# Cross-attention with a small expert layer: where the key weights are split, six stage slots for the last key tiles, waits per bank and per block

## The reference, cut to what matters

```python
q = (layernorm(x) @ Wq + bq).reshape(B, L, NKV, G, HDIM)     # 8 groups of 4 heads, width 128
k_, v_ = jnp.split(ctx @ Wkv + bkv, 2, axis=-1)              # 8 key/value heads
scores = jnp.einsum('blkgd,bmkd->bkglm', q, k) * scale       # each block of 64 sees its own 64
o = jnp.einsum('bkglm,bmkd->blkgd', softmax(scores), v)
x = x + o @ Wo + bo
x = x + top-2-of-8 experts of rank 16 (layernorm(x)) * 0.5
```

## Time and profile before

| what | value |
|---|---|
| timed runs | 1084.54, 1086.21, 1086.89 us (median 1086.21) |
| profiled execution | span 1083.3 us, first to last instruction; the profile has no other time of it |
| TensorE busy | 1043.1 us, 96% of the span |
| VectorE, GpSimd, ScalarE busy | 807.1 us (75%), 674.0 us (62%), 556.9 us (51%) |
| chain that ended last | TensorE 83%, VectorE 7%, DMA 5%, GpSimd 2% |
| slices of the span with TensorE below 8 tenths | the first and the last |
| DMA | 183 GB/s on average, up to 327 GB/s in a slice of the start |

### The profile page before, as it was taken

The page is one execution under the profiler, slowest core; times in us unless marked ns, Lnnn a source line. Parts: engine busy times, 40 slices in busy tenths (PEclk is TensorE's granted clock), DMA queues, the critical chain, the costliest instruction groups (busy, mean ns, idle before and its releaser), DMA issues.

```text
span 1083.3 us, 17308 instructions
## 1 busy us (share of the span) xinstructions
PE 1043.1 (96%) x5409; PEld 856.0 (79%) x5409; DVE 807.1 (75%) x1420; ACT 556.9 (51%) x1314; POOL 674.0 (62%) x563
## 2 busy tenths in 40 slices
PE   7999899888999999999999999999999999999996
PEld 6788687776778888888888888888888888887884
DVE  3554355446997798788879887887888797788886
ACT  3032203225775675667566656756666665566420
POOL 0285235766886787578667866876786678575300
PEclk9999999988999999999999999999999999999998
DMA  8636863875654637273635637282736456350003
GB/s 300 194 121 205 327 185 110 312 248 214 223 199 161 243 108 292 97 288 111 246 141 209 231 127 254 97 321 93 261 138 221 161 194 250 103 156 11 2 37 120
DMA packets 85658, 197.99 MB, mean 183 GB/s; under 512 B 10561, under 2 KB 43369, under 8 KB 70385
## 3 DMA queue, kind: packets, MB, share of 16 engines
q1 hardware_dynamic: 83072, 181.73, 48.1%
q10 hardware_dynamic: 2544, 15.73, 3.7%
HBM read 161.78 MB, written 35.65 MB: 182 GB/s over the span
## 4 chain that ended last, share of the span: by engine, by line
PE 83%; DVE 7%; DMA 5%; POOL 2%; SPq 1%; ACT 1%; issue 1%; DVEq 0%; ACTq 0%
PE banks L1633 25%; PE banks L1634 23%; PE banks L1635 23%; PE banks L1773 5%; PE banks L1756 3%; PE banks L1757 3%; DMA raw<-in_L_xattn_Wkv_dram 2%; DMA keys_dram<-parts 1%; PE banks L1658 1%; DMA xo<-x_dram 1%; DVE stats L1193 1%; DVE xo L1118 1%; SPq L402 1%; DMA v_raw<-values_dram 1%; DVE y L1313 1%
## 5 line engine op out<-in xcount | busy, mean ns | idle before, releaser
L1633 PE MATMUL banks<-wo_h,xo 128*128 128x512 f32 x512 | 204.5, 399 | 0.0
L1634 PE MATMUL banks<-wo_l,xo 128*128 128x512 f32 x512 | 200.4, 391 | 0.0
L1635 PE MATMUL banks<-wo_h,xo 128*128 128x512 f32 x512 | 199.8, 390 | 0.0
L562 POOL TENSOR_TENSOR qT_l<-parts,qT_h 128x512 fp32r<-128x512 f32 x128 | 165.3, 1298 | 46.8 <-ACT qT_h L784 46.8
L1633 PE MATMUL banks<-xo,w_h 128*128 128x512 f32 x448 | 180.5, 403 | 12.2 <-DVE parts L1157 6.8
L1634 PE MATMUL banks<-xo,w_h 128*128 128x512 f32 x448 | 177.0, 395 | 0.0
L1635 PE MATMUL banks<-xo,w_l 128*128 128x512 f32 x448 | 175.7, 392 | 0.0
L562 POOL TENSOR_TENSOR xo<-sT,xo 128x512 fp32r<-128x512 f32 (+1 forms) x72 | 102.4, 1423 | 75.5 <-ACT xo L784 75.5
L1266 DVE SCALAR_TENSOR_TENSOR parts<-banks,g_bias,parts 128x512 f32<-128x512 f32 x128 | 94.8, 742 | 37.5 <-PE banks L1635 33.8
L1118 DVE TENSOR_TENSOR xo<-banks,xo 128x512 fp32r<-128x512 f32 (+1 forms) x156 | 100.8, 665 | 24.9 <-ACT xo L784 24.4
L1633 PEld LDWEIGHTS banks<-wo_h,xo 128*128 128x128 f32 x512 | 96.4, 188 | 23.3 <-issue 0.2
(11 more groups left out here) (145 smaller groups left out, 2281.6 us busy)
## 6 DMA issues: line engine op xcount, KB each, us to landing
xo<-x_dram SPq DMA_DIRECT2D x105, 1024.0 KB, 5.0
x_dram<-xo ACTq DMA_DIRECT2D x14, 1024.0 KB, 11.2
values_dram<-parts SPq DMA_DIRECT2D x64, 128.0 KB, 2.5
keys_dram<-parts SPq DMA_DIRECT2D x32, 256.0 KB, 3.5
k_raw<-keys_dram SPq DMA_DIRECT2D x32, 256.0 KB, 4.0
raw<-in_L_xattn_Wo_dram SPq DMA_DIRECT2D x8, 1024.0 KB, 8.0
v_raw<-values_dram SPq DMA_DIRECT2D x64, 128.0 KB, 3.4
raw<-in_L_xattn_Wkv_dram SPq DMA_DIRECT2D x7, 1024.0 KB, 6.2
```

Of the source, the lines that this page charges most:

```text
L562: return nc.gpsimd.tensor_tensor(dst, src, high_part.bitcast(F32), ALU.subtract)
L1633: mm(dst, stat[0], mov[0], start=start, stop=False)
L1634: mm(dst, stat[0], mov[1], start=False, stop=False)
L1635: return mm(dst, stat[1], mov[0], start=False, stop=stop)
```

## The change

1. **Key weights.** In steps 0 and 2 ScalarE splits them at V(j,4), two tiles later; steps 1 and 3 stay at V(j,2). SyncE issues step 2's load of the key weights ahead of the loads of x tiles 0 to 3.
2. **Stage slots.** The last eight key units, step 3's, use slots 3, 4, 6, 2, 0, 1, 3, 4 of `parts` in place of 0 to 2 in turn (slots 3 and 4 held the value bias, which is used no more by then). Every slot has a semaphore.
3. **Per bank.** The start's units are moved by three ring banks, so that the last four end in banks 0 to 3, and each first product waits for its own bank. ScalarE and VectorE wait, each in front of the instruction that overwrites a slot, for that slot's store.
4. **Blocks.** Each block has its own semaphore; blocks are stored in the order 0, 2, 1, 3, 6, 4, 5, and SyncE has an opening of its own, in which the loads of duo 1's blocks wait for the stores of the same block and for the product that used the buffer last.
5. **Small moves.** The first key load goes to the begin of step 3's key units; ScalarE's value copy goes behind two query copies, the key copy and a piece of the output weights; six additions of `residual` on GpSimd go in between the `differences`.

```diff
-                elif name[0] == "V" and name[2] == 2:
+                elif name[0] == "V" and name[2] == (2 if name[1] % 2 else 4):
...
+                    if name == ("V", 2, 0):
+                        sp.wait_ge(tile_filled, tile_no["c", 11] + 1)
+                        for t in range(0, 4):
+                            load_x(t)
+                    if name == ("K", STEPS - 1, 0, 0):
+                        m = kv_no["K", 0, 0, 0]
+                        sp.wait_ge(kv_stored[kv_slot[m]], kv_value[m])
+                        load_keys(0, 0, 0)
...
+        LAST_SLOTS = (3, 4, 6, 2, 0, 1, 3, 4)
+        kv_slot = [m % SLOTS for m in range(len(kv_order) - len(LAST_SLOTS))] + list(LAST_SLOTS)
...
+            return (n - FIRST_UNIT) % RING
...
-                    pe.wait_ge(ring_emptied, FIRST_UNIT)
+                    pe.wait_ge(ring_emptied, FIRST_UNIT - RING + 1 + n)
...
-                        store_block(1 if step == 1 else 0, i, 4 if step == 1 else 8)
+                        store_block(1 if step == 1 else 0, (0, 2, 1, 3, 6, 4, 5)[i], 4 if step == 1 else 8)
...
+            def opening():
+
+                load_wo(wo_v[:, 0:G, :], QLOWS + OPS)
+                for k, op in ((1, 0), (6, 2), (2, 1), (7, 3)):
+                    sp.wait_ge(block_stored[op], 16 * DUOS)
+                    load_block(1, op, PROD_AT[k, 1] + 1)
+                    if op == 0:
+                        sp.wait_ge(resid_ready, TILES)
+                        load_values(0, 0, 0)
+                load_keys(0, 1, 1)
+                for op in (4, 5, 6):
+                    sp.wait_ge(block_stored[op], 16 * DUOS)
+                load_block(1, 5, len(PROD) + PROD_AT[1, 1] + 1)
+                load_values(0, 1, 1)
+                load_block(1, 4, len(PROD) + PROD_AT[6, 1] + 1)
+                load_block(1, 6, len(PROD) + PROD_AT[2, 1] + 1)
+                for t in kv_stored:
+                    sp.wait_ge(kv_stored[t], stored[t])
+                load_keys(0, 2, 2)
...
-                for m in range(len(kv_order) - SLOTS, len(kv_order)):
-                    act.wait_ge(kv_stored[m % SLOTS], kv_value[m])
+                act.wait_ge(kv_stored[0], stored[0])
                 first_product(0, 0, 0)
+                act.wait_ge(kv_stored[1], stored[1])
                 first_product(0, 0, 1)
-                values_high(0)
-                query_high(0, "c11", 0)
                 keys_high(0)
-                split_wo(STEPS, [0])
+                query_high(0, "c11", 0)
                 query_high(0, "c11", 1)
+                split_wo(STEPS, [0])
+                values_high(0)
...
+                dve.wait_ge(kv_stored[2], stored[2])
                 y_sum(0, 0, 0)
+                dve.wait_ge(kv_stored[3], stored[3])
                 y_sum(0, 0, 1)
...
+                dve.wait_ge(kv_stored[4], stored[4])
                 z_sum(0, 0, 0, 0)
```

More of the change, by code:

```diff
@@ L228, in build @@
         c_loaded = [sem(f"c_loaded{t}") for t in range(PTILES)]
-        kv_stored = [sem(f"kv_stored{t}") for t in range(SLOTS)]
-        blocks_stored, out_stored = sem("blocks_stored"), sem("out_stored")
+        kv_stored = {t: sem(f"kv_stored{t}") for t in (0, 1, 2, 3, 4, 6)}
+        block_stored = [sem(f"block_stored{op}") for op in range(OPS)]
+        out_stored = sem("out_stored")
         block_loaded = [sem(f"block_loaded{b}") for b in range(XBUFS)]
@@ L483, in load_block, with duo @@
                              ).then_inc(block_loaded[BUF_OF[op]], 16)
-            def duo(g, p, first):
+            def opening():
[16 more added lines that the diff above has]
+                load_keys(0, 2, 2)
+                load_w(STEPS + 1, wq_v, G * HD)
+                load_keys(0, 3, 3)
+                load_block(0, 0, len(PROD) + PROD_AT[4, 1] + 1)
+                load_block(0, 2, len(PROD) + PROD_AT[5, 1] + 1)
+                load_values(0, 2, 2)
+                load_block(0, 1, len(PROD) + PROD_AT[3, 1] + 1)
+                load_block(0, 3, len(PROD) + PROD_AT[3, 1] + 1)
+                load_keys(1, 0, 4)
+            def duo(g, p):
                 d = g * DUOS + p
@@ L524, in duo @@
                     load_block(1 - p, 2, product(5))
-                if not first:
-                    load_values(g, 2 * p, 2 * d)
+                load_values(g, 2 * p, 2 * d)
                 if not last:
@@ L755, in _ @@
             split_wv(3)
+            residual(0)
+            residual(4)
             differences(4)
             split_wo(3, range(KC))
-            for i in range(5, 8):
-                differences(i)
+            differences(5)
+            residual(1)
+            differences(6)
+            residual(5)
+            differences(7)
+            residual(2)
+            residual(6)
             split_q(0, list(USE_OF), True)
-            for t in (0, 4, 1, 5, 2, 6):
-                residual(t)
             opening()
@@ L822, in tile_high @@
                     if i == 4:
-                        act.wait_ge(blocks_stored, 16 * OPS)
+                        for op in range(OPS):
+                            act.wait_ge(block_stored[op], 16)
                     high(xo[:, 0:2, 0, :, cols], src.rearrange("p (o k) n -> p o k n", o=2)).then_inc(x_high, 1)
@@ L926, in opening @@
                 query_high(1, "c11", 0)
[L927 removed]
+                act.wait_ge(block_stored[6], 16 * DUOS)
                 probs_high(0, 0)
@@ L931, in opening @@
                 query_high(1, "c11", 1)
+                for op in (4, 5):
+                    act.wait_ge(block_stored[op], 16 * DUOS)
                 output_high(0, 0, 0)
@@ L1152, in keys_or_values @@
                 if name[0] == "V":
-                    ins = nc.vector.tensor_tensor(kv_stage[:, m % SLOTS, :], ring[:, n % RING, :],
+                    ins = nc.vector.tensor_tensor(parts[:, kv_slot[m], :], ring[:, start_slot(n), :],
                                                   bv_bc[:, chunk * D:(chunk + 1) * D], ALU.add)
@@ L1156, in keys_or_values @@
                     head = NH + chunk * KVH + name[3]
-                    ins = nc.vector.tensor_scalar(kv_stage[:, m % SLOTS, :], ring[:, n % RING, :], bias[:, head:head + 1],
+                    ins = nc.vector.tensor_scalar(parts[:, kv_slot[m], :], ring[:, start_slot(n), :], bias[:, head:head + 1],
                                                   None, ALU.add)
@@ L1688, in values @@
                         pe.wait_ge(w_low, step * KC + c + 1)
-                    last = passes(ring[:, n % RING, :], (tokens_h[:, c], tokens_l[:, c]), (wv_h[:, c, :], wv_l[:, c, :]),
+                    last = passes(ring[:, start_slot(n), :], (tokens_h[:, c], tokens_l[:, c]), (wv_h[:, c, :], wv_l[:, c, :]),
                                   c == 0, c == KC - 1)
@@ L1700, in keys @@
                         pe.wait_ge(wo_low, step * KC + c + 1)
-                    last = passes(ring[:, n % RING, :], (wo_h[:, c, cols], wo_l[:, c, cols]),
+                    last = passes(ring[:, start_slot(n), :], (wo_h[:, c, cols], wo_l[:, c, cols]),
                                   (cT[b][0][:, c, :], cT[b][1][:, c, :]), c == 0, c == KC - 1)
@@ L1707, in warm @@
                 for _ in range(times):
-                    mm(ring[:, RING - 1, 0:P], ident[:], ident[:], start=True, stop=True)
+                    mm(ring[:, start_slot(RING - 1), 0:P], ident[:], ident[:], start=True, stop=True)
             def product(g, p, k, r):
@@ L1920, in _ @@
                     pe.wait_ge(bias_loaded, 48)
-                    nc.tensor.transpose(ring[:, n % RING, 0:rows], bias_rows, ident[0:rows, 0:rows]).then_inc(ring_filled, 1)
+                    nc.tensor.transpose(ring[:, start_slot(n), 0:rows], bias_rows, ident[0:rows, 0:rows]).then_inc(ring_filled, 1)
                 elif kind == "V":
```

99 lines of the change are left out of this document (43 added, 56 removed).

## The result

The changed kernel ran in 1071.34 us (median of four, 1070.41 to 1071.81), the kernel before on the same chip in 1086.03 us: ratio 0.9871, interval 0.9852 to 0.9889. That is 14.7 us faster; 20.9 us were forecast (1065.3 us), and the time lies inside the range. The profiled execution has a span of 1068.2 us, 15.1 us less than before.

The account below looks back on a forecast made before the run. TensorE was busy nearly all the time, so gains could only be its pauses. 2.9 + 5.9 + 0 + 5.1 + 7.0 = 20.9 us off 1086.2 gave 1065.3 us, range a little below 1061.4 to 1073.

Parts of the forecast that it names:

- Step 0: Opening step: splitting key weights two tiles later ends V(0,4)'s pause, leaves 2.1 us at V(0,5); 2.9 us gained.
- Step 2: At V(2,6): earlier weight load and later split remove the 4.18 us pause and 1.7 us of low clock; 5.9 us.
- Residual additions: GpSimd's moved additions, eight taking 9.83 us, mostly placed where GpSimd idles: taken as 0 us.
- First products and scores: Opening: products start at once, slots' stores then delay some, scores start at 235.2 and not 240.31; 5.1 us.
- Duo 1's block: Duo 1's product on a loaded block: earlier load removes the 5.37 us pause and some 1.7 us low clock; 7.0 us.
- Behind that nothing: After duo 1's block product: no pauses counted on that the change reaches.
- new pauses pull the clock down: Rival, step 0 and first products: two of four new pauses cost 1.7 to 2.1 us each; 1069.1 us, chance 0.11.
- No slot holds: Rival, first products: no slot's store delays them, 9.0 us for 5.1; 1061.4 us, chance 0.09.
- stores land together: Rival, first products: all slot stores land with the last, 1.7 us for 5.1; 1068.7 us, chance 0.12.

Follow-up runs that it names:

- block stores after keys: Changed kernel with the last three 1 MB block stores issued by ScalarE behind the first two product copies and the key copy: 1072.46 us, ratio 0.9892.
- three slots: Changed kernel with step 3's last eight key units using slots 0 to 2 in turn again: 1074.08 us, ratio 0.9893.
- key load ahead of blocks: Changed kernel with the third unit's keys loaded before the three loads of duo 1's last blocks again: 1075.20 us, ratio 0.9911.
- statistics later: Changed kernel with layer-norm statistics of x8 behind c7's low part, x12's behind V(0,7), and an output-weight split before GpSimd's roots: 1064.82 us, ratio 0.9823.
- the fastest kernel: Changed kernel with step 0's layer-norm statistics moved back, the value copy behind c21's query copies and the first key load at V(3,2): 1060.71 us, ratio 0.9777.
- first key load earlier: Changed kernel with the first key load issued at V(3,2), not at the begin of step 3's key units: 1070.53 us, ratio 0.9865.

## Why the prediction was right or wrong

The direction and the places were right; the gain came out 5.8 us too large by the spans (20.9 against 15.1). By the prediction's own steps:

- **Step 0: 2.9 forecast, 1.25 measured.** The new pause ends where it was put (27.37; 27.4 forecast) and for the reason given: x8 landed at 23.3, where 23.4 was taken. A value store, which the forecast left out, ended VectorE's addition at the same moment. The step that failed is "2.1 is nearer to 1.54, which didn't, than to 4.18, which did". The pause was 2.58 us, since V(0,4) began at 21.35 and not at 22.2, and behind it the clock fell, 1.7 us: V(0,7) begins at 36.66 and not at 35.0, 1.66 later. Part of the mistake was in the reading of before: only 35 to 40 us were looked at there, but behind that step's first pause, 3.19 us, the clock had been at 0.66. How often the place costs this, other runs show. In seven traces with this step 0 the pause is 1.15 to 2.67 us. In the five with over 2.1 us the clock fell; in block stores after keys (1.15 us) and three slots (1.88 us) it didn't, and V(0,7) began at 33.72 and 34.52, earlier than forecast.
- **Step 2: 5.9 forecast, 5.84 measured.** No pause, clock 1.00. That the two agree to 0.1 us is luck: between the same two places the five traces with equal lists gain 3.3 to 6.0 us. Two edits were given one answer; the run with the old order of loads showed that the split's place is enough.
- **Residual additions: 0, as measured.** No wait of TensorE in the list after is put down to them.
- **First products and scores: 5.1 forecast, 2.62 measured.** They begin at once, as said. Then the terms of the slots were too small: the fifth product came 8.15 us behind the first and not 6.5, the sixth 11.9 and not 9.5. The first store took 10.3 us (10.1 taken from the earlier trace rows) but was issued 1.1 us later than forecast, and the next, issued at 203.70, let ScalarE go on at 217.06, after 13.4 us and not 12.3. What set the scores was the values' load. It was given 0.8 us ("behind 2 MB, so I give it 0.8 us, 231.4"); in the time of before it landed for the copy at 226.81 + 7.1 = 233.9, 2.5 us later, and the scores were 2.5 us later than forecast, at 237.7 and not 235.2. The step that failed is that 0.8 us: the load took 14 us, and it stood behind two 1 MB loads and beside block stores, which no run tells apart. With the value copy out of the way the scores were 22.1 us behind the first product, where 22.2 were forecast; that these agree is chance, since the forecast had the values set them. With the block stores behind the copies too it was 17.7.
- **Duo 1's block: 7.0 forecast, 6.84 measured.** No wait for a block, none for VectorE in its place.
- **Behind that nothing: 1.45 us lost.** "Behind that I count on none that the change reaches" failed. The pause of 1.97 us at the outputs was there before, without cost to the clock; now 1.98 us cost 1.45. Nine of the fourteen traces have that fall and five don't, so it isn't shown that the change brought it on.

So of the 5.8 us, 1.7 and 1.5 are the granted clock behind a pause, and 2.5 the time of the values' load. The rival "new pauses pull the clock down" was half right: the price was right (1.7 us each), the place was one of its four and one old pause. "No slot holds" fell, since two waits at the products were over 2 us, and so did "stores land together", since the two copies went on 3.9 us apart.

## What to carry to other kernels

When a transfer holds an engine, ask what lies ahead of it in its own queue and beside it in the others between its issue and its landing: key stores of 256 KB took 8 to 14 us beside 1 MB stores and 4 to 7 us without. A wait taken from one instruction of an in-order engine passes to the next, unless the late thing is moved to the end of what needs nothing from it. A context tile's low part, on which TensorE waits, belongs ahead of statistics that nobody waits for yet: that one move gained 5.2 us by the ratios. And here a pause between 2 and 3 us should be priced with and without the fall of the clock, old pauses behind the change included.

## What was not expected of the hardware

Equal pauses of TensorE were followed by different clocks (all of this from 14 to 320 us of each trace). The pause at the outputs, 1.97 to 2.00 us, is in all fourteen traces: in five the granted clock behind it was 1.00 (before, key load ahead of blocks, three slots, statistics later, and the fastest kernel), in nine it fell for part of the next 5 us. The other pauses from 1.96 to 2.87 us went both ways too: 2.39, 2.55, 2.76 and 2.80 us were followed by 1.00, but 2.12, 2.14 and 2.21 us by 0.50, 0.63 and 0.69 in the next 2.5 us. Those of 3.19 us and more were followed by the low clock each time (eight of them), and those from 1.1 to 1.88 us never, except one right behind a pause of 2.47 us. The Trainium skill (TensorE: Matmul & The Clock Gate, What's actually happening) says that the window over which TensorE's activity is watched runs free and does not start over with the kernel; by that, where a pause falls in it could decide, and the traces agree in that a pause's length alone didn't. The times spread with the mean granted clock: with the old order of loads 1070.03 us at 0.992 and 1076.6 at 0.987, with the first key load earlier 1068.94 at 0.995 and 1072.35 at 0.990.
